# Attention batches of a transformer block: norm applications, negated maxima and the rounding of rotated rows on ScalarE instead of VectorE

## What is computed

```python
x = x + 0.5 * ffn(layernorm(x))        # mixture of experts: top 2 of 8, 128 -> 512 -> 128, gelu, then a layer norm
x = x + attention(layernorm(x))        # 16 heads of 8, rotary positions, softmax over 256 keys
x = x + 0.5 * ffn(layernorm(x))
```

## Time and profile before

| | |
|---|---|
| median of 3 runs | 566.41 us (565.49 to 566.83) |
| time of the profiled execution | 566.3 us |
| its span in the trace | 564.3 us |
| busy: PE / PEld / DVE / ACT / POOL | 449.0 / 372.4 / 364.8 / 277.6 / 224.8 us |
| attention's exponentials | first starts at 209.7 us, last at 391.9 us |

### The profile page before, as it was taken

One profiled execution on the slowest core, in us unless ns is written; L12 is line 12 of the kernel. 1 busy time (PEld: TensorE's weight loads), 2 busy tenths in 40 slices (PEclk: granted clock), 3 DMA queues, 4 the chain that ended last, 5 costly groups with the idle time before them and its releaser, 6 DMA issues. The chain is left out here.

```text
span 564.3 us, 11026 instructions
## 1 busy us (share of the span) xinstructions
PE 449.0 (80%) x3428; PEld 372.4 (66%) x3428; DVE 364.8 (65%) x1139; ACT 277.6 (49%) x571; POOL 224.8 (40%) x280
## 2 busy tenths in 40 slices
PE   1724896999899977898888988786996899999920
PEld 0723685888799865676665766654796788888820
DVE  4676444344876758999999998822364554677446
ACT  1322456465466444656656566454553455555500
POOL 3278586273444221220223323203345484354321
PEclk9999998799999985979979799785897999999975
DMA  9342424112221000000000000301111231221231
GB/s 289 131 117 69 135 67 124 50 48 81 72 66 39 25 20 19 20 1 21 21 9 11 11 13 19 81 11 39 44 43 48 62 110 48 85 85 49 71 93 38
DMA packets 35512, 33.62 MB, mean 60 GB/s; under 512 B 5681, under 2 KB 29873, under 8 KB 35265
## 3 DMA queue, kind: packets, MB, share of 16 engines
q1 hardware_dynamic: 30000, 22.24, 14.4%
q0 software_dynamic: 4992, 10.27, 5.4%
q10 hardware_dynamic: 464, 0.41, 0.3%
HBM read 21.59 MB, written 15.27 MB: 65 GB/s over the span
## 5 line engine op out<-in xcount | busy, mean ns | idle before, releaser
L470 POOL DMA_INDIRECT expert_y<-stage x92 | 91.1, 990 | 136.5 <-DVE stage L1506 122.5
L1115 ACT ACTIVATE stage<-ps 128x512 f32<-128x512 f32 x92 | 54.9, 597 | 118.2 <-PE ps L691 117.1
L1498 DVE TENSOR_TENSOR ring_hi<-ps,ring_hi 128x512 fp32r<-128x512 f32 x92 | 63.5, 691 | 40.0 <-ACT ring_hi L1122 39.6
L1608 DVE TENSOR_REDUCE mx<-ps 128x4 f32<-128x1024 f32 x64 | 77.2, 1214 | 10.7 <-PE ps L796 10.2
L1492 DVE TENSOR_TENSOR bx<-ps,bx 128x128 fp32r<-128x128 f32 x92 | 26.5, 288 | 82.3 <-ACT bx L1098 81.1
L1167 ACT ACTIVATE stage<-ps 128x1024 f32<-128x1024 f32 x64 | 65.4, 1022 | 28.7 <-PE ps L807 27.6
L714 PE MATMUL ps<-w_hl,ring_hi 128*128 x276 | 78.2, 352 | 1.2 <-DVE stage L1506 1.2
L715 PE MATMUL ps<-w_hl,ring_hi 128*128 x368 | 72.5, 238 | 0.0
L715 PEld LDWEIGHTS ps<-w_hl,ring_hi 128*128 128x128 f32 x368 | 65.0, 194 | 0.0
L449 POOL DMA_INDIRECT sorted_x<-rows,place_at x32 | 31.8, 994 | 70.7 <-DVE place_at L1391 64.4
L700 PE MATMUL ps<-const,stage 128*128 128x128 f32 x368 | 57.5, 279 | 0.5 <-DVE ring_hi L1498 0.4
(11 more groups left out here) (172 smaller groups left out, 1054.1 us busy)
## 6 DMA issues: line engine op xcount, KB each, us to landing
stage<-sorted_x SPq DMA_DIRECT2D x92, 64.5 KB, 1.9
stage<-w SPq DMA_DIRECT2D x16, 256.0 KB, 6.8
y_got<-expert_y SPq DMA_DIRECT2D x24, 128.0 KB, 2.3
sorted_x<-padding SPq DMA_DIRECT2D x4, 516.0 KB
sorted_x<-padding SPq DMA_DIRECT2D x28, 64.5 KB
expert_y<-stage POOLq DMA_INDIRECT x92, 2.3
x_tok<-x SPq DMA_DIRECT2D x4, 256.0 KB, 5.2
sorted_x<-rows,place_at POOLq DMA_INDIRECT x64, 2.4
```

The lines of the kernel that those rows point to most:

```text
L470: gp.indirect_dma_start(expert_y, bass.IndirectOffsetOnAxis(ap=x_rows[:, n % XB, D:D + 1].bitcast(U32), axis=0), y_rows[:, n % YB, :], Non ...
L1115: act.activation(g_full[:, s, :], ps[:, H_BANK, :], ACT.Gelu).then_inc(g_done, 1)
L1498: vec.tensor_tensor(bg_lo[:, s, :, :].rearrange("p c n -> p (c n)"), ps[:, G_BANK, :], bg_hi[:, s, :, :].rearrange("p c n -> p (c n)").bit ...
L1608: vec.tensor_reduce(mx[:, t, :].rearrange("p (r g j) -> p r j g", r=2, g=2)[:, pair, 2 * jp:2 * jp + 2, :], ps[:, at:at + 2, :].rearrange( ...
```

## The change

Three kinds of work go from VectorE to ScalarE inside the attention batches:

- both negations of the maxima (for the sequences 1 to 7);
- the attention norm's application for the sequences 3 to 7 (one batch later than before, near the start of ScalarE's batch), and the second mixture's norm application for the sequences 0 to 6;
- the rounding of the rotated rows for the sequences 2 to 7.

ScalarE computes `scale * x + bias`, so the bias `-mean * rstd` is made by two further small GpSimd operations for each norm. GpSimd gets a wait before it overwrites `rstd` (the earlier application must be over), and VectorE a wait before the maxima 0 and 4 of a sequence overwrite `mx` (the earlier negation must be over). VectorE keeps the statistics.

```diff
@@ GpSimd
+            def att_bias_of(i):
+                gp.wait_ge(att_norm[2], 2 * i + 2)
+                gp.tensor_tensor(att_bias[:, :], mv[:, :, 0], rstd[:, :], ALU.mult).then_inc(att_bias_steps, 1)
+                gp.wait_ge(att_bias_steps, 2 * (i - 3) + 1)
+                gp.tensor_scalar(att_bias[:, :], att_bias[:, :], -1.0, None, ALU.mult).then_inc(att_bias_steps, 1)
+            def pre_bias_of(c):
+                ... (the same with fmv, frstd and pre_bias)
@@ GpSimd, batch
                     pre_rstd(FIRST_UNIT + b - 1)
+                    pre_bias_of(b - 1)
                 if more:
                     low_rotated(b + 2, p)
                 if norm:
                     post_rstd_of(b + 3)
+                    if b >= 1:
+                        gp.wait_ge(a_ln_done, b + 3)
                     att_rstd(b + 3)
+                    att_bias_of(b + 3)
@@ ScalarE
+            def negate_late(b, pair):
+                act.wait_ge(max_done, SU * b + 4 * pair + 4 + MAX_BUF)
+                act.activation(shift_v[:, :, 8 * pair:8 * pair + 8, 24:25].rearrange("p t h c -> p t (h c)"),
+                               mx[:, :, 8 * pair:8 * pair + 8], ACT.Copy, scale=-1.0).then_inc(shift_ready, 1)
+            def a_apply(b):
+                act.wait_ge(att_bias_steps, 2 * (b - 3) + 2)
+                for t in range(BT):
+                    op = act.activation(xn[:, t, :], x_tok[:, b * BT + t, :], ACT.Identity,
+                                        bias=att_bias[:, t:t + 1], scale=rstd[:, t:t + 1])
+                op.then_inc(a_ln_done, 1)
+            def apply_late(c):
+                act.wait_ge(pre_bias_steps, 2 * c + 2)
+                for t in range(c * BT, c * BT + BT):
+                    op = act.activation(rows1[:, t, 0:D], x_tok[:, t, :], ACT.Identity,
+                                        bias=pre_bias[:, t:t + 1], scale=frstd[:, t:t + 1])
+                op.then_inc(ln_done, 1)
+            def rot_high(b, p):
+                act.wait_ge(rot_sum, b + 1)
+                act.activation(rot_hi[:, p, :, :], rot, ACT.Copy).then_inc(rot_hi_done, 1)
@@ ScalarE, batch
                 if place_next:
                     copy_placed(b + 1, q, 2, M0)
+                if b >= 1:
+                    negate_late(b, 1)
+                if b >= 1 and project_next:
+                    a_apply(b + 2)
                 exps(b, 1)
                 copy_shifted(b, 1)
...
                 exps(b, 4)
+                if place_next:
+                    negate_late(b + 1, 0)
                 exps(b, 5)
                 if place_next:
                     copy_shifted(b + 1, 0)
                 exps(b, 6)
+                if project_next:
+                    rot_high(b + 2, p)
                 copy_weighed(b, 0)
                 if place_next:
                     copy_values(b + 1, q)
+                if tail:
+                    apply_late(b - 1)
                 exps(b, 7)
@@ VectorE
-                vec.wait_ge(rot_sum, b + 1)
-                vec.tensor_copy(rot_hi[:, p, :, :], rot).then_inc(rot_hi_done, 1)
+                if b < 2:
+                    vec.wait_ge(rot_sum, b + 1)
+                    vec.tensor_copy(rot_hi[:, p, :, :], rot).then_inc(rot_hi_done, 1)
...
+                    if b >= 2 and u % 4 == 0:
+                        vec.wait_ge(shift_ready, 2 * (b - 1) + u // 4 + 1)
@@ VectorE, batch
                     maxima(b + 1, 3)
-                    negate(b + 1, 0)
...
                     maxima(b + 1, 7)
-                    negate(b + 1, 1)
-                if norm:
-                    a_norm(b + 3, stats_part=False)
-                if tail:
-                    pre_apply(FIRST_UNIT + b - 1)
```

More of the change, by code:

```diff
@@ L189, in build @@
         mx = sb("mx", [P, BT, HEADS])
+        att_bias = sb("att_bias", [P, BT])
+        pre_bias = sb("pre_bias", [P, TILES])
         rden = sb("rden", [P, HEADS])
@@ L266, in build @@
         att_norm = sem("att_stats"), sem("att_var_ready"), sem("att_rstd_ready")
+        att_bias_steps, pre_bias_steps = sem("att_bias_steps"), sem("pre_bias_steps")
         rot_sum, rot_hi_done, rden_ready = sem("rot_sum"), sem("rot_hi_done"), sem("rden_ready")
@@ L411, in att_rstd @@
                 gp.tensor_tensor(rstd[:, :], rstd[:, :], neg_half[:, 0:BT], ALU.pow).then_inc(rstd_ready, 1)
+            def att_bias_of(i):
[4 more added lines that the diff above has]
+            def pre_bias_of(c):
+                u = FIRST_UNIT + c
+                first, many = unit_tiles(u)
+                t = slice(first, first + many)
+                gp.wait_ge(rstd_ready, 2 * u + 2)
+                gp.tensor_tensor(pre_bias[:, t], fmv[:, t, 0], frstd[:, t], ALU.mult).then_inc(pre_bias_steps, 1)
+                gp.wait_ge(pre_bias_steps, 2 * c + 1)
+                gp.tensor_scalar(pre_bias[:, t], pre_bias[:, t], -1.0, None, ALU.mult).then_inc(pre_bias_steps, 1)
             def pre_rstd(u):
```

## The result

The changed kernel takes 571.99 us (median of 6, 570.68 to 574.01), the kernel before 566.62 (median of 6): ratio 1.0099, 95% interval 1.0075 to 1.0122. The forecast was 571.5 us, slower than before. The profiled execution took 571.86 us with a span of 570.1, 5.8 more than before. The ratios are formed from the undisturbed executions and are not the ratios of the medians that stand beside them, so the two can differ by some tenths of a per cent.

The account below looks back on a forecast made before the run. VectorE bounds mainly at batch 3's start (1.47 us), elsewhere the ScalarE and TensorE chain does; additions less VectorE's relief sum to 5.3 us on 566.3, giving 571.6, stated as 571.5. Range 568.5 to 574, with B and C 566 to 576.

Parts of the forecast that it names:

- What bounds the kernel: Attention batches: VectorE late only at batch 3's start, 1.47 us, and 0.23 in batch 4; elsewhere waits name ScalarE.
- Term (1), late pair: Second mixture's norm application, two activations before exponential 7 on ScalarE: 0.69 us each in six batches, hidden in batch 7.
- Term (2), early pair: Second negation and attention norm's two activations before exponential 1, batches 1 to 5: place(b+1, 3) 0.55 us late.
- Terms (3) to (5): First negation before exponential 5, rounding behind exponential 6, waits on GpSimd and VectorE: hidden; rounding 0.5 us per batch if uncovered.
- VectorE's `gap`: VectorE's subtraction beside GpSimd's low_rotated: later rounding moves the stall to another operation or none, 0 to 1.0 us relief.
- The sum: Batches 1 to 6: ScalarE's additions less VectorE's lateness give 5.3 us more, low bounds 3.3, high 7.5.
- The clock: TensorE's fall to 1.2 GHz: one stretch may come or go, 2 us either way; left open.
- A: VectorE is the pace; batches 1 to 5 each shorter by its relief, 5 x 1.74 = 8.7 us, 557.7 us; 14 in 100.
- B: ScalarE's additions absorbed by cheaper pairs and VectorE's late pieces in batches 3 and 4: 566 to 567 us; 10 in 100.
- C: Additions as forecast plus two more lower-clock stretches, in batches 2 and 5: 575.5 us; 11 in 100.

Follow-up runs that it names:

- run 5: Kernel before, with VectorE's two norm applications and rounding writing 8 columns instead of 128 or 256, ScalarE given nothing: 576.62 us, before 577.94, ratio 0.9997.
- run 1: Changed kernel with the second mixture's norm application back on VectorE: 565.25 us, kernel before 566.0, ratio 1.0014.
- run 4: Changed kernel with second mixture's norm application moved on ScalarE from before exponential 7 to behind exponential 0 of next batch: 566.17 us, before 566.0, ratio 1.0019.
- run 3: Changed kernel with both norm applications back on VectorE, negations and rounding staying on ScalarE: 564.62 us, kernel before 566.0, ratio 0.9976.
- run 7: Changed kernel with second mixture's norm application behind next batch's exponential 0 and attention norm's application back on VectorE: 575.55 us, before 577.94, ratio 0.9962.
- run 9: Changed kernel with mixture's norm application behind next exponential 0, attention norm's application and second negation back on VectorE: 575.92 us, before 577.41, ratio 0.9976.
- run 2: Changed kernel with the attention norm's application back on VectorE: 571.38 us, kernel before 566.0, ratio 1.0113.
- run 10: Changed kernel itself, measured again on the second chip: 581.52 us, kernel before 577.41, ratio 1.0065.
- run 6: Changed kernel with a second, spare pair of activations in front of the second mixture's norm application, batches 1 to 6: 590.38 us, kernel before 577.94.
- run 8: Kernel before with only the rounding of the rotated rows moved to ScalarE: 577.33 us, kernel before 577.94, ratio 0.9942.

## Why the prediction was right, point by point

**What bounds the kernel.** Right in the main. VectorE, with the highest share but one, set the pace around batch 3 (its steps there were 1.16 us longer, the end of batch 2 was 0.39 longer: 1.55 for a forecast of 1.47). For the batches 4 and 5 I read its lateness too small from the waits that the timeline prints. The waits were 0.23 us and none; the steps were 0.49 and 0.13 longer than in b1. `place` (L787) normally starts 0.41 us after the transposes (L877) in front of it, and in b4 and b5 it started 0.88 and 0.53 after them (307.52 to 308.40 and 331.42 to 331.95):

```profile
307.52 0.66 PE L877 MATMUL ps<-const,arena 128*128 128x128 f32 x4 [0.23 <-ACT ring_lo L1161]
...
331.95 0.39 PE L787 MATMUL ps<-x_hi,sel_r 128*128 128x256 f32 x1
```

In all VectorE's lateness was worth 2.2 us at the upper clock, and the changed kernel gains all of it. No run takes the whole work off VectorE without giving it to ScalarE; run 5, meant for that, takes off less than a third. ScalarE's order decides (runs 1 and 4).

**Term (1), late pair.** Forecast 0.69 in six batches, 4.1 us. A pair takes 0.77 us of the queue (forecast 0.75; one activation 0.48, forecast 0.49), and its cover was 0.15 instead of 0.06, since the copy of the values had overlap to give: 0.62 at the upper clock, 3.7 us. The estimate of 0.77 for the pair from the figures of the Trainium skill ("ScalarE: Activation LUTs", What ACT_TABLE_LOAD costs) is what the trace shows. In batch 7 the pair is hidden, as forecast: ScalarE's next work follows 399.13 - 397.49 = 1.64 us after the start of the exponential, where it was 2.27.

**Term (2), early pair.** Forecast 0.55, measured 0.55 (6.85 to 7.40), but its parts were wrong. I had the negation's hold on place_shifted at nothing and the delayed exponential alone responsible. The negation costs 0.18 to 0.2 by itself: place_shifted starts 0.62 us after the transposes in front of it (330.30 to 330.92) where it started 0.41 after them (329.19 to 329.60 in batch 5 before), because it waits for the negation (over at 330.77), which stands in ScalarE's queue behind the very copy that releases TensorE; before, VectorE had made the negated maxima by 328.12. Runs 3, 7 and 9 show it (7.04, 7.04, 6.86). The pair adds 0.36. For batch 6, where only the negation is added, I had counted nothing; it is 0.2.

**Terms (3) to (5)**, first negation, rounding, waits on GpSimd and VectorE: hidden, as forecast. For the negation and the rounding run 3 shows it; for the waits, the changed kernel's trace, in which no wait of GpSimd names an application on ScalarE and none of VectorE a negation. The rounding takes 0.63 us in front of a wait that shrank from 1.14 to 0.62.

**VectorE's `gap`.** The stall went where the Trainium skill ("SBUF — State Buffer", Who interferes with whom) lets it go, to another VectorE operation with two inputs in SBUF. VectorE's `gap` and the second pair of combine's operations, then GpSimd's remainder, batch 4 after:

```profile
320.89 0.16 DVE L1417 TENSOR_TENSOR gap<-top 128x2 f32<-128x2 f32 x1
...
322.61 1.51 DVE L1603 SCALAR_TENSOR_TENSOR y_got<-y_got,share 128x128 f32<-128x128 f32 x2
```

```profile
322.25 1.45 POOL L484 TENSOR_TENSOR x_lo<-arena,x_hi 128x512 fp32r<-128x512 f32 x1 [2.89 <-ACT x_hi L1226]
```

`gap` takes 0.16 instead of 1.18 us, and two operations that take 0.61 together in batch 4 before (at 322.16) take 1.51. No wait in the trace names them. So semaphores are not the only thing that ties two engines together here.

**The sum.** At the upper clock, from the steps: the first three 0.54 + 0.55 - 0.61 + 0.06 + 0.42 + 0.20 = 1.16 for b1 to b6 (the lower clock's 1.65 in b3 and 1.57 in b6 taken out), the end of batch 2 -0.41, the late pair 6 x 0.62 = 3.72: 4.5 us. The forecast for the same was 5.3. Of the 0.8 too much, the late pair in five batches is 0.35 (0.62 for 0.69 each), VectorE's greater lateness in the batches 4 and 5 is 0.4, the stretch from batch 2's late pair through batch 3 is 0.3 (-0.4 for -0.1), and batch 6's negation takes 0.2 back. From the first exponential of batch 0 to ScalarE's first work of the experts the profiled attention is 189.95 - 184.52 = 5.4 us longer. So the forecast 5.3 met the total because a sum 0.8 too large stood beside a clock term of about 1 us that I had put at zero. That the total came within 0.5 us is luck; that the order of ScalarE's queue costs some 5 us is not.

**The clock.** Held open with 2 us either way, and it stays the open part. In the profiled executions the lower level holds for these times (us) in the batches 1 to 6; the prediction had left batch 6 out:

| | b1 | b2 | b3 | b4 | b5 | b6 | all |
|---|---|---|---|---|---|---|---|
| before | 6.8 | 3.4 | 6.8 | 6.8 | 0 | 10.2 | 34.0 |
| changed | 3.4 | 0 | 10.2 | 3.4 | 0 | 13.6 | 30.6 |

So the changed kernel has less of it, and it lies elsewhere: less in the middle of batches, and new at the start of the batches 3 and 6, over the weighted sum behind the 1.68 us wait, where it costs most, 1.6 us for 3.4. The profiled execution of run 1 has 37.4 us of it and is 7.8 us shorter than that of the changed kernel. So the sum of the time at the lower level does not explain the order of the kernels; where it falls matters too.

The first weighted sum of a batch tells whether it falls there: it takes 1.93 us at the upper level and 3.1 to 3.6 at the lower. In the batches 1 to 6, each of the four profiled kernels that keep the late pair at its place has at least one long one: the changed kernel in b3 and b6, run 2 in b2, run 10 in b2 and b5, run 6 in b2, b4, b5 and b6. None of the eight others has one, on either chip. So the lower level comes to the start of a batch with the late pair, where TensorE waits 1.68 us or more instead of 1.06. How much of the total this makes is not shown. Taking the pair out gives 6.1 us by medians, 5.3 at equal mean clock and 4.8 by the ratios, for 3.7 in the steps; putting a second one in costs 8 for 4.6, in a run that scatters by 16. Both lean the same way, but neither excess is clear of the scatter.

Some first steps on the other chip are longer for another reason: by 0.9 to 1.45 us in b4 or b5 of the runs 5, 7, 8 and 9. There the granted clock is 1.0 and the weighted sum takes its 1.93 us, but ScalarE's copy of it starts 1.1 to 1.7 us after its end instead of 0.07. Run 9, batch 4:

```profile
303.43 1.93 PE L888 MATMUL ps<-stage,arena 128*32 128x256 f32 x32
```

```profile
306.62 0.60 ACT L1192 ACTIVATE arena<-ps 128x512 f32<-128x512 f32 x1 [1.30 <-PE ps L888]
```

What held it, no row says.

**The rivals.** A fell with the steps, which show 2.2 us of VectorE's lateness where A needs over 5, and with run 4. B came out for no edit with the late pair in place. C, two more stretches with a total of 575.5, came half true: two stretches of 3.4 us did appear at new places (batches 3 and 6, not 2 and 5), while one of 3.4 went and two of 6.8 became half as long.

## What to carry to other kernels

A full engine and an empty one are no reason to move work: ask which instruction the moved one will stand in front of, and who waits for that one. The same 0.77 us, six times, cost 4.5 to 6 us in front of an exponential on the chain and nothing that could be measured some 4 us later, behind the next exponential, in a wait of 0.88 us (runs 1 and 4). Two conditions of a third engine that were fulfilled side by side on two engines become a sum when both are put into one queue, even if the second is only 0.2 us long. An edit that is to take work away must be measured by what it takes: on 8 columns instead of 128 an operation of VectorE kept 0.29 of its 0.345 us (run 5). Per-step intervals of a loop, compared at equal clock, resolve hundredths of a microsecond where the total scatters by several.

## What was not expected of the hardware

- One kernel's time moved with the mean granted clock by 3.0 us per 0.01 on the first chip: 561.4 to 567.8 us for the same program. Small gains drown in it; the versions of the runs 3, 7, 8 and 9 cannot be told apart.
- With the late pair in front of exponential 7 TensorE waits 1.68 us instead of 1.06 once per batch (longer with the pair twice), and in all four profiled kernels of this kind the lower clock then lies over the matmuls right behind at least one such wait: 32 of them take 3.44 us instead of 1.93. It does so in none of the eight others.
- The second chip takes 11 us more for the kernel before (577.4 to 577.9 for 566.0), and the differences between kernels are of the same size there.
